# Another order for the router's turns, gathers and weight loads, and the odd table's last block summed in SBUF

## What is computed

```python
router_logits = x @ gate_w                       # 64 experts in 8 groups
topk_w, topk_ids = _grouped_topk(router_logits, bias)   # best 4 groups, best 6 experts
y = _routed_moe(x, topk_w, topk_ids, w_gate, w_up, w_down)  # at most 96 tokens an expert
shared = jax.nn.silu(x @ ws_gate) * (x @ ws_up) @ ws_down
return (y + shared).reshape(orig_shape)
```

## Time and profile before

| | |
|---|---|
| median of three runs | 1073.44 us |
| the profiled execution | 1077.39 us, its span 1075.6 us |
| TensorE busy | 962.3 us (89%) |
| VectorE, GpSimd, ScalarE busy | 657.7, 639.4, 400.4 us |
| this block begins | 641 us |
| first expert product (L1707) | 731.98 us |
| last expert product ends (L1726) | 1034.6 us |
| the last scatter has landed | 1043.9 us |
| last DMA packets | between 1071 and 1072 us |

### The profile page before, as it was taken

The page is one execution under the profiler, slowest core; times in us unless marked ns, Lnnn a source line. Parts: engine busy times, 40 slices in busy tenths (PEclk is TensorE's granted clock), DMA queues, the critical chain, the costliest instruction groups (busy, mean ns, idle before and its releaser), DMA issues. The chain is left out here.

```text
span 1075.6 us, 13598 instructions
## 1 busy us (share of the span) xinstructions
PE 962.3 (89%) x4376; PEld 471.0 (44%) x4398; DVE 657.7 (61%) x1204; ACT 400.4 (37%) x805; POOL 639.4 (59%) x565
## 2 busy tenths in 40 slices
PE   5879999669999999799999998958999999999981
PEld 4445544324444444344444444314555555555530
DVE  6679888968888887677777777951222222222220
ACT  4334544334444444566666654221111111111110
POOL 4496887558888886786777650252445554444431
PEclk9989999879999999999999999988999999999996
DMA  7654555340000001500004204158999999999548
GB/s 256 233 137 118 128 118 137 55 131 2 1 1 1 1 2 40 191 25 20 21 20 155 100 33 163 59 196 307 337 335 338 332 339 339 337 341 337 132 64 175
DMA packets 63796, 162.90 MB, mean 151 GB/s; under 512 B 9920, under 2 KB 10064, under 8 KB 63152
## 3 DMA queue, kind: packets, MB, share of 16 engines
q1 hardware_dynamic: 46960, 115.89, 30.9%
q0 software_dynamic: 16640, 41.95, 18.0%
q10 hardware_dynamic: 128, 4.19, 1.1%
HBM read 129.67 MB, written 40.72 MB: 158 GB/s over the span
## 5 line engine op out<-in xcount | busy, mean ns | idle before, releaser
L579 POOL TENSOR_TENSOR ARENA<-ARENA 128x512 f32<-128x512 f32 x128 | 133.4, 1063 | 54.2 <-DVE ARENA L822 54.1
L1418 POOL DMA_INDIRECT out<-ARENA,idx x32 | 46.0, 1437 | 133.8 <-DVE ARENA L1571 129.0
L1005 PE MATMUL PS<-SLAB,ARENA 128*128 128x512 bf16 x497 | 116.5, 382 | 8.3 <-DVE ARENA L773 5.1
L1829 ACT ACTIVATE ARENA<-PS 96x192 f32<-96x192 f32 x64 | 20.9, 327 | 228.2 <-PE PS L1707 143.1
L1571 DVE COPY ARENA<-PS 96x512 f32<-96x512 f32 x64 | 41.1, 681 | 94.6 <-PE PS L1726 94.6
L1226 ACT ACTIVATE ARENA<-PS,ARENA 128x512 f32<-128x512 f32 x128 | 86.9, 683 | 23.6 <-DVE ARENA L816 20.3
L1707 PE MATMUL PS<-SLAB,ARENA 128*96 128x384 f32 x240 | 82.9, 499 | 0.0
L816 DVE TENSOR_REDUCE ARENA<-PS 128x2 f32<-128x1024 f32 x64 | 78.2, 1222 | 6.9 <-PE PS L1039 6.5
L1005 PEld LDWEIGHTS PS<-SLAB,ARENA 128*128 128x128 bf16 x512 | 48.9, 98 | 68.1 <-issue 13.6
L1050 PEld LDWEIGHTS PS<-ident,ARENA 128*128 128x128 f32 x512 | 54.8, 141 | 51.1 <-issue 35.0
L1192 ACT ACTIVATE ARENA<-PS 128x512 f32<-128x512 f32 x64 | 38.2, 597 | 103.2 <-PE PS L1005 84.6
(11 more groups left out here) (265 smaller groups left out, 1845.4 us busy)
## 6 DMA issues: line engine op xcount, KB each, us to landing
SLAB<-in_L_ffn_w_gate SPq DMA_DIRECT2D x30, 384.0 KB
SLAB<-in_L_ffn_w_up SPq DMA_DIRECT2D x30, 384.0 KB
X<-in_L_ffn_w_down SPq DMA_DIRECT2D x14, 768.0 KB
SLAB<-in_L_ffn_w_down SPq DMA_DIRECT2D x10, 768.0 KB
CT<-in_L_ffn_w_gate SPq DMA_DIRECT2D x16, 384.0 KB
CT<-in_L_ffn_w_up SPq DMA_DIRECT2D x16, 384.0 KB
X<-in_ctx SPq DMA_DIRECT2D x4, 1024.0 KB, 5.4
XNT<-in_L_ffn_w_gate SPq DMA_DIRECT2D x16, 256.0 KB
```

The source lines that it names most:

```text
L579: last = pool.tensor_tensor(prob[s % 4][:, h, :], prob[s % 4][:, h, :], rec[:, s % 4, h:h + 1].to_broadcast([P, D]), ALU.mult)
L1005: last = pe.matmul(bank(b), QT[:, par, k * P:(k + 1) * P], w[:, k, c * D:(c + 1) * D], start=(k == 0), stop=(k == KD - 1))
```

## The change

- Tiles 0 to 9 are turned before `logits(0)`, 10 to 12 before `turn_logits(0)`, 13 to 15 behind it; ScalarE's copies follow (`turn_rows_x`, `columns_out`).
- Of group 1 the long product is first and the short one behind `turn_keys`. `ORDER` goes.
- `turn_halves` stands behind `shared_two(2, 0)`.
- `sh` has four buffers, so `shared_out` waits for `into_x` two tiles later; `hs[0]` moves to `CT`.
- `into_x(8)` and `(9)` come after gathers 0 and 1, `(10)` and `(11)` after gathers 2 and 3.
- SP loads pair 2 after tile 3's store has landed, and pair 4 right behind.
- In the tail, SP reads the last four tiles' rows of `odd_sum` into SBUF (`odd_l`, in `SLAB`), VectorE adds the scaled shared product to them from PSUM, and GpSimd accumulates the sum into `out` with two DMAs of two tiles. The 1 MB accumulate from `odd_sum`, its wait and ScalarE's copies go.

```diff
         ub = arena(SW)
-        sh = arena(2 * D).rearrange("p (m d) -> p m d", m=2)
-        hs = [arena(SW), ct_flat[:, 3 * T + NE:3 * T + NE + SW]]
+        sh = arena(KD * D).rearrange("p (n d) -> p n d", n=KD)
+        hs = [ct_flat[:, 2 * T + NE:2 * T + NE + SW], ct_flat[:, 3 * T + NE:3 * T + NE + SW]]
         flip = arena(CAP)
...
         NS = NT - KD
-        ORDER = [(0, 1), (1, 0), (0, 1), (0, 1)]
...
-            return 2 * g + ORDER[g].index(m) + 1
+            return 2 * g + m + 1
...
                              "o_ready", "merged"))
-        merged_l, shared_added = sem("merged_l"), sem("shared_added")
+        odd_in, shared_added = sem("odd_in"), sem("shared_added")
...
         ssil_l, ub_l, hs_l = arena(SW), arena(D // 2), arena(SW)
-        sh_l = arena(KD * D).rearrange("p (n d) -> p n d", n=KD)
+        odd_l = SLAB[:, 0:KD * D].rearrange("p (n d) -> p n d", n=KD)
         assert used[0] <= ROUTE
...
                     sp.dma_start(out_v[:, i, :], X[:, i, :]).then_inc(acc_stored[(i + 4) // 8], 16)
-                    if i == 7:
+                    if i == 3:
                         sp.wait_ge(acc_stored[0], 64)
                         load_pair(sp, 2)
-                    if i == 8:
                         sp.wait_ge(sgu_done, 2 * (GCH - 1))
...
                     load_pair(sp, t, gu6_done, y6_done)
+                sp.wait_ge(gu6_done, 2 * (PAIRS // PW * PW) + 2)
+                sp.wait_ge(added[1], 16 * PAIRS)
+                sp.dma_start(odd_l, odd_sum[NS * P:T, :].rearrange("(n p) d -> p n d", p=P)).then_inc(odd_in, 16)
...
                 def shared_product(g):
-                    for m in ORDER[g]:
+                    for m in range(2):
                         pool.wait_ge(ssil_ready, up_count(g, m))
...
                     pool.wait_ge(sh_ready, i + 1)
-                    pool.tensor_tensor(X[:, i, :], X[:, i, :], sh[:, i % 2, :], ALU.add).then_inc(acc_ready, 1)
+                    pool.tensor_tensor(X[:, i, :], X[:, i, :], sh[:, i % KD, :], ALU.add).then_inc(acc_ready, 1)
...
-                into_x(NS - 4)
-                into_x(NS - 3)
                 pool.wait_ge(idx_ready, 1)
...
                 gather(1)
+                into_x(NS - 4)
+                into_x(NS - 3)
+                gather(2)
+                gather(3)
                 into_x(NS - 2)
                 into_x(NS - 1)
-                for e in range(2, GR):
+                for e in range(4, GR):
                     gather(e)
...
                     pool.wait_ge(added[n], 16 * PAIRS)
-                pool.dma_start(out[NS * P:T, :], odd_sum[NS * P:T, :], accum_op=ALU.add, max_dma_last_dim=4 * 4 * D).then_inc(merged_l, 16)
                 pool.dma_start(out[0:NS * P, :], odd_sum[0:NS * P, :], accum_op=ALU.add, max_dma_last_dim=4 * 4 * D).then_inc(merged, 16)
-                pool.wait_ge(merged_l, 16)
-                for n in range(KD):
-                    pool.wait_ge(sh_ready, NS + n + 1)
-                    pool.dma_start(out_v[:, NS + n, :], sh_l[:, n, :], accum_op=ALU.add).then_inc(shared_added, 16)
+                for n in range(0, KD, 2):
+                    pool.wait_ge(sh_ready, NS + n + 2)
+                    pool.dma_start(out_v[:, NS + n:NS + n + 2, :], odd_l[:, n:n + 2, :], accum_op=ALU.add).then_inc(shared_added, 16)
                 pool.wait_ge(merged, 16)
-                pool.wait_ge(shared_added, 16 * KD)
+                pool.wait_ge(shared_added, 16 * KD // 2)
             @block.vector
...
                 dve.tensor_tensor(hs_l[:, D:SW], ssil_l[:, D:SW], ub_l, ALU.mult).then_inc(hs_ready, 1)
+                dve.wait_ge(odd_in, 16)
+                for n in range(KD):
+                    dve.wait_ge(sd_done, NS + n + 1)
+                    dve.scalar_tensor_tensor(out=odd_l[:, n, :], in0=bank((2, 3, 4, 5)[n]), scalar=tgate[:, 3:4], in1=odd_l[:, n, :],
+                                             op0=ALU.mult, op1=ALU.add).then_inc(sh_ready, 1)
             @block.tensor
...
-                def turn_four(g):
-
-                    for i in range(4 * g, 4 * g + 4):
+                def turn_rows_x(low, high):
+
+                    for i in range(low, high):
                         pe.wait_ge(xn_ready, i + 1)
...
-                turn_four(0)
-                turn_four(1)
-                turn_four(2)
+                turn_rows_x(0, 10)
                 pe.wait_ge(bias_in, 32)
                 logits(0)
-                turn_four(3)
+                turn_rows_x(10, 13)
                 turn_logits(0)
+                turn_rows_x(13, NT)
                 logits(1)
...
                 shared_up(0, 1)
+                shared_up(1, 0)
+                turn_keys()
                 shared_up(1, 1)
-                turn_keys()
-                shared_up(1, 0)
                 for two in range(2):
...
                     shared_two(1, two)
+                shared_two(2, 0)
                 turn_halves()
-                shared_two(2, 0)
                 pe.wait_ge(iota2_set, 2)
...
-                def columns_out(g):
-                    for i in range(4 * g, 4 * g + 4):
+                def columns_out(low, high):
+                    for i in range(low, high):
+                        g = i // 4
                         act.wait_ge(xn_turned, i + 1)
...
-                columns_out(0)
-                columns_out(1)
-                columns_out(2)
+                columns_out(0, 10)
                 logits_out(0)
-                columns_out(3)
+                columns_out(10, 13)
                 scores_out(0)
+                columns_out(13, NT)
                 logits_out(1)
...
                         act.wait_ge(sd_done, i + 1)
-                        need(act, acc_ready, i - 1)
-                        act.activation(sh[:, n % 2, :], bank((4, 5, 2, 3)[n]), ACT.Copy, scale=tgate[:, 3:4]).then_inc(sh_ready, 1)
+                        need(act, acc_ready, i - 3)
+                        act.activation(sh[:, n, :], bank((4, 5, 2, 3)[n]), ACT.Copy, scale=tgate[:, 3:4]).then_inc(sh_ready, 1)
...
                 shared_hidden(0, 1)
-                shared_hidden(1, 1)
+                shared_hidden(1, 0)
                 for r in range(4):
...
                 keys_out(1)
-                shared_hidden(1, 0)
+                shared_hidden(1, 1)
                 shared_out(0)
...
                 last.then_inc(ub_ready, 1)
-                for n in range(KD):
-                    act.wait_ge(sd_done, NS + n + 1)
-                    act.activation(sh_l[:, n, :], bank((2, 3, 4, 5)[n]), ACT.Copy, scale=tgate[:, 3:4]).then_inc(sh_ready, 1)
```

## The result

The changed kernel took 1060.28 us (median of four runs, 1056.12 to 1061.55) beside 1074.09 for the kernel before; the ratio is 0.9861, with a 95% interval of 0.983 to 0.9893. By the medians the change is worth 13.8 us in one comparison and 18.8 in the other, by the ratios 14.9 and 18.4. The forecast was 1056.9, with a range of 1053.5 to 1063.0.

A forecast was written before the change was run, and what follows sets the result against it. Bounds: the router's wait chain through TensorE and VectorE, a rigid TensorE-bound expert loop, a tail of accumulating packets. Front 13.9 plus tail 2.6 gives 16.5 us: 1077.39 to 1060.9 profiled, less 3.95 for the median, 1056.9 (1053.5 to 1063.0).

The forecast's parts named there:

- Turns and keys: Router: earlier first logits, then a new wait for the keys; extraction starts 1.9 us sooner (1.2 to 2.3).
- The list's turn: Router's end: the column transpose no longer waits behind a shared down product on TensorE; 3.9 us gained (3.5 to 4.0).
- The port: Before the gathers: two VectorE operations of 1.18 us return to about 0.2 without GpSimd's product beside them; 1.95 us gained.
- Gathers: Before the expert loop: with loads moved away, gathers take 4.0 us and gather 1 lands 5.2 us sooner (1.6 to 5.7).
- the rival of slow gathers: Router's end: gathers take 7.6 us or more even in quiet, through their indirect form; 1061.5 us, chance 0.14.
- The clock: First expert product: shorter TensorE idling before it keeps the clock higher; 1.0 us gained, between 0 and 2.1.
- The loop: Expert loop: moves as a rigid block, its weight loads keeping up with 12 us in hand; cost 0.
- The tail: After the last scatter: a plain read and VectorE additions replace a 1 MB accumulate; the end comes 2.6 us earlier.
- the read's head start: Tail: SP's read has 1 us alone, 190 packets, before GpSimd's merge packets begin.
- The alternation: Tail: beside the 3 MB merge, queues share one packet for one, so small read packets pay for large ones.
- the sign given for this step: Tail: last scatter to last packet takes 25 us, not 28, with queue 1's packets spread over most of the merge.
- The sum: Whole kernel: 13.9 us at the front plus 2.6 at the end, 16.5 us, giving 1056.9 us.

The follow-up runs named there:

- b_loads: Kernel before with only the loads of pairs 2 and 4 issued at result tile 3 instead of tiles 7 and 8: 1070.61 us beside 1075.93, ratio 0.9931.
- after_again: The changed kernel timed and profiled once more, with no edit: 1058.41 us beside 1077.25 for the kernel before, ratio 0.9829.
- b_halves: Kernel before with only the turn of the list's halves put behind the shared down product (2, 0): 1070.71 us beside 1075.93, ratio 0.9946.
- a_fill: Changed kernel plus 16 and 5 idle transposes on TensorE around the turn of gather 0's rows: 1058.68 us beside 1077.25, ratio 0.9821.
- a_read_late: Changed kernel with SyncE's tail read held until the last block's second shared down product is done: 1064.68 us beside 1075.93, ratio 0.9882.

## Why the prediction was right, and where its steps were off

The mechanisms were the foreseen ones, and the four parts taken alone add up: span less the first turn's start falls from 433.9 us to 432.5, 427.0, 428.3 and 429.3 with one part each, together 18.5 us, and to 416.1 and 415.4 with all, 17.8 and 18.5. (The fallen clock takes 0.8 us from `b_loads` and 1.1 from the first of the two. The four buffers of `sh` and the result tiles behind the gathers are in none of the four and were never run alone.) The working of each step:

- **Turns and keys, 1.9 us.** The step that VectorE gets its keys late and that the extraction starts behind the key copies was right, and so was that `shared_up(1, 0)` sets them. Its size is 2.5 us with the clock whole: counted from the first turn, `after_again` reached the keys after 35.6 us, where the sum had 36.0, and the extraction began 2.1 us later, where it had 2.4. It was 1.4 between the two first profiles only because the clock fell at 642 in the one after. That fall wasn't in the sum at all; it costs 1.1 us of the forty turns and can hit either kernel. The range given, 1.2 to 2.3, was too short on the upper side.
- **The list's turn, 3.9 us.** From the list's arrival to the end of the column transpose 1.2 us instead of 5.2: 4.0.
- **The port, 1.95 us.** The six small operations took 1.35 us instead of 3.23: 1.9, and `b_halves` ties it to `into_x`.
- **Gathers, 5.2 us.** 3.38 instead of 9.23, so 5.85; the 4.0 that was taken was a little long, and the rival of slow gathers is out (`b_loads`). The Trainium skill's page "DMA: Bandwidth & Descriptors", section "Anatomy of one DMA", gave an estimate of 2.5 us; the 3.2 to 4.2 us that these gathers took with the loads moved lie above it. (The prediction says that the trace has nothing so short. Of gathers that is so; an 8 KB load took 1.7 us.)
- **The clock, 1.0 us.** Wrong: nothing came back. TensorE idled 2.44 us for gather 0, the clock was at 0.50 by 718, and the first eight took 4.76 us, 0.3 more than before. The step read one idle gap of 2.7 us that left the clock whole as if such gaps always did; in five of the thirteen profiles it fell after just that gap. `a_fill` shows that 2.2 us lie there and that they aren't worth as much at the end.
- **The loop, 0.** A rigid block of 297.5 us in the kernel after, 0.7 shorter than before. `a_fill` limits the statement: with the fill the same loop took 1.8 to 3.6 us more, waiting for rows and not for weights.
- **The tail, 2.6 us.** Right in its direction, 4.1 in size (3.9 to 4.3). The step that failed is the read's head start, taken as 1 us; it was 3.4, from 1030.3 to 1033.7, so the read was alone for nearly all of its 512 packets. Its root is a reading of the trace before. The 1043.87 that stands in the table and in the prediction as the landing of the last scatter is GpSimd's next issue. The scatters' last packets are sooner, in 1041 to 1042:

```profile
q0 software_dynamic: 50, 0.07, 40.2%
```

From 1042 to 1045 no packet moves at all. In the kernel after, SyncE issued its read 4.3 us after the issue of the last scatter (1024.91), GpSimd its merge 6.1 us after it, as before (6.0). Those 1.8 us belong to GpSimd and not to the scatter. The alternation that the sum used is real (`a_read_late`), but was hardly entered; and the sign given for this step, queue 1's packets spread over most of the merge, did not appear.

The sum, 16.5 us, stands against 17.3 between the first two spans and 19.4 to the second. That it lies so near the 17.3 is partly luck: in that pair the turns gave 0.5 less (the fallen clock), the clock before the product 1.3 less and the block began 0.5 later, while the gathers gave 0.65 more, the loop 0.7 and the tail 1.7. The time that it was turned into, 1056.9, was 3.4 below the measured 1060.28 although the gain was underrated, and the last step did that: from the profiled execution to the median 3.95 us were taken off because three runs of the kernel before had a median of 1073.44. In the later comparisons its medians were 1075.93, 1077.25 and 1076.76 (33 runs, 1072.9 to 1079.2), so the profiled 1077.39 was an ordinary run and those three were low. From the middle one of these medians the same sum gives 1076.8 - 16.5 = 1060.3; that this is the measured time to the digit is chance, since the two medians of the kernel after are 1.9 us apart. A large part of this spread lies in front of the change: the router's first turn is between 637.07 and 642.46 in the thirteen profiles. Between the kernel before and `b_halves`, whose code is the same until the router, it is 3.8 us, and most of that is there by 194 us, as TensorE's timelines of the two show:

```profile
193.78 3.70 PE L959 MATMUL PS<-CT,XNT 128*128 x8 [0.15 <-ACT XNT L1130]
```
```profile
190.04 3.69 PE L959 MATMUL PS<-CT,XNT 128*128 x8 [0.15 <-ACT XNT L1130]
```

Where it arises before that wasn't followed.

## What to carry to other kernels

Before a short latency-bound transfer on which an engine waits, look at what else is issued at that time: moving bulk loads off it took 6 us from a gather of 9. Two queues that take turns by single packets, as these did, make a transfer of small packets pay for large ones beside it, so start it first: ahead of the merge the read took 5.3 us, within it 14.0. And when single runs of one kernel differ by more than the effect, cut the profiles at common points and compare the stretches.

## What the hardware did that was not expected

TensorE's clock fell or held at the same place in the same code: after an idle gap of 2.67 us it was 0.50 in one profile of the kernel after and 1.00 in the next, worth 1.1 us over forty turns. Gap and work were equal, so neither alone decides it.

GpSimd's DMA comes later than SyncE's behind the same scatters: 1.8 us between the issues at 1029.21 and 1031.01. (GpSimd waits for both tables' scatters and SyncE for the odd ones alone, but all their packets had gone by 1029.) Then a queue that comes second waits for its first packet. SyncE's came 1.1 us after its issue when it was first and 3.7 when the merge was in flow; GpSimd's came 1.7 and 1.8 us after when it was first (`a_read_late`, before) and 2.7 beside the read. What holds it wasn't looked into.

A faster first product did not shorten what follows: with the first product at 2.58 us instead of 4.76 the loop took 1.8 to 3.6 us longer.
